# The split of the rows for hop 3, done by groups of five tiles inside the tail of the first feed-forward stage

## The chip, the core and the metric

The kernel runs on one core of a Trainium2 chip. The metric is the device time of one execution in microseconds (us). A core has TensorE (PE: products of 128x128 weights with a moving operand, into the banks of PSUM), VectorE (DVE), ScalarE (ACT), GpSimd (POOL) and SyncE (SP), which here issues nearly all transfers. Each engine works through its own instructions in the order in which they were written. What one engine needs of another it waits for on a counter, a semaphore.

## What is computed

Two layers of a network over a graph with 3125 nodes of 256 features and 53125 edges. Each layer adds to a stream x a hop over the graph and an attention, then a feed-forward part; the second layer's hop is a plain sum over neighbours. Cut to the place that matters, from the first layer's feed-forward to the second layer's first hop:

```python
x = x + L0_ffn(layernorm(x))          # two experts, GELU, then its own layernorm
xn = layernorm(x)
# second layer, on xn
agg = segment_sum(xn[src], dst)       # hop 3
h = (1 + eps1) * xn + agg
h = relu(relu(h @ W1a + b1a) @ W1b + b1b)
h = (1 + eps2) * h + segment_sum(h[src], dst)       # hop 4
gnn = relu(h @ W2a + b2a) @ W2b + b2b
mix = linear_attention(rmsnorm(xn) @ w_qkv)          # queries and keys pass a softmax
x = x + gnn + mix
x = x + L1_ffn(layernorm(x))          # six experts
```

## The kernel before

**Tiles.** The nodes are cut into T = 25 tiles of 128 rows, and these into five groups of GROUP = 5 tiles. X holds the stream, N the normalised rows (both tile by tile), NT the normalised rows transposed.

**The end of the feed-forward stage.** TensorE runs the second expert products group by group (line 972, 80 matrix instructions a group, 16 a tile), into two PSUM banks in turn (the object V over TV). VectorE empties a bank with an addition into N (`accumulate`, line 1699) and by that gives it back. VectorE's loop at line 1808 is the tail, with steps s = 0 to 6. In step s it normalises group s - 2 into N (`normalised`, counted by `xn_ready`), empties group s's banks, takes group s - 1 through a layer norm and into the stream (`into_stream`, four parts between the five emptyings) and makes group s's statistics. Each layer norm needs a root of ScalarE, which VectorE asks for at the end of a step.

**Transposes.** `normalised_transposed(2, g)` on TensorE turns the five tiles of group g through three PSUM banks (TA). ScalarE copies each into NT (line 1208, counted by `nt_ready`) and then rounds the group to bf16 into hi16 (`leading_part`, line 1269, counted by `hi_ready`). Groups 0 and 1 are turned between the expert products, groups 2 to 4 at line 980, all of them before hop 3.

**The split.** Hop 3 is a dense product with an adjacency matrix in bf16; to keep fp32's accuracy each row is the sum of three bf16 parts: hi16, and two parts in both16, which lies over N itself. For tile t VectorE subtracts hi16 from N into one of three buffers (`remainder`, line 1913, `rest_ready`), GpSimd casts that into both16 (line 774, `mid_ready`), and VectorE subtracts the cast and writes the last part (`low_part`, line 1905, `lo_ready`). Since both16 overwrites N, GpSimd first waits until N has gone to DRAM (`table_written[2]`, five stores of SyncE), until ScalarE has squared all rows for the attention's norms (`norm_asked`; line 1295, 25 squares, then a root at line 1299) and until all tiles are transposed. `split_rows` is one run over 25 tiles. Ahead of it VectorE scales NT into the sums' rows AT (line 1953) and adds N into X (line 1958).

**Hop 3.** `dense_products` runs 40 pieces: 8 slabs of target nodes by 5 groups of source tiles. A piece is two halves (c = 0, 1) of fifteen matrix instructions (line 1062), and needs the three parts of its group. Lists of steps, `beside_pieces`, are worked off between the halves: for tile t of the attention, queries, keys and values (line 990) beside piece t, and the turn of the normalised queries (line 997) beside piece t + 1. VectorE has a list of its own, by piece: the norms (`over_norm`, line 1825), the normalising of queries, and at each slab's end the addition of the two banks into AT (line 1933), on which TensorE's next slab waits. SyncE loads pieces into four buffers.

Two passages that set the order (SyncE's loads and stores, and GpSimd's waits):

```python
            for i in range(4):
                load_piece(i)
            for g in range(GROUPS):
                sp.wait_ge(xn_ready, 2 * T + (g + 1) * GROUP)
                load(sp, rows_of_table(2, g * GROUP, (g + 1) * GROUP), N[:, g * GROUP:(g + 1) * GROUP, :], table_written[2])
...
            pool.wait_ge(table_written[2], 16 * TABLE_DMAS[2])
            pool.wait_ge(norm_asked, 1)
            pool.wait_ge(nt_ready, 3 * T)
```

Of the kernel before, what the change touches and what calls it, by code (L numbers as in the profile page):

```python
# [29 lines left out]
ALU = mybir.AluOpType  # L30
# [25 lines left out]
GROUP = 5  # L56
# [55 lines left out]
def build(nc, a, out):  # L112
    with ExitStack() as ctx:
# [3 lines left out]
        def sem(name):  # L117
            return ctx.enter_context(nc.semaphore(name))
# [65 lines left out]
        table_sbuf = [sem(f"table_sbuf{h}") for h in range(4)]  # L184
        table_written = [sem(f"table_written{h}") for h in range(3)]
        row_stored = [sem(f"row_stored{i}") for i in range(4)]
        hidden_hi, hidden_rest, hidden_mid, hidden_lo = sem("hidden_hi"), sem("hidden_rest"), sem("hidden_mid"), sem("hidden_lo")
# [29 lines left out]
        def load(eng, dst, src, s):  # L217
            eng.dma_start(dst, src).then_inc(s, 16)
# [91 lines left out]
        V_B3 = V_GNN1 + T  # L310

        EARLY = 9
        A_W1B = A_MIX1 + 2 * T + 2 * SLICES * HC + EARLY
# [42 lines left out]
        def rows_of_table(i, first, last):  # L356
            return table[i][first * P:last * P, :].rearrange("(t p) d -> p t d", p=P)
# [13 lines left out]
        def _(sp):  # L371
# [38 lines left out]
            load(sp, beta_b, a["L0_ffn_beta"].partition_broadcast(P), b2_loaded)  # L410
            sp.wait_ge(pv_full, V_FFN0)
            load(sp, WA[:, 0:1024], a["w1a"], w1_loaded)
            sp.wait_ge(slab_stored, 16 * SLABS)
            def load_piece(i):
                load(sp, pieces[i % 4], adjacency[i // GROUPS][:, GROUP * (i % GROUPS):GROUP * (i % GROUPS + 1), :], piece_loaded[i % 4])

            for i in range(4):
                load_piece(i)
            for g in range(GROUPS):
                sp.wait_ge(xn_ready, 2 * T + (g + 1) * GROUP)  # L420
                load(sp, rows_of_table(2, g * GROUP, (g + 1) * GROUP), N[:, g * GROUP:(g + 1) * GROUP, :], table_written[2])
            for i in range(4, PIECES):
# [80 lines left out]
        def gather_general(pool, h):  # L503


            if h < 4:
                pool.wait_ge(table_written[h - 1], 16 * TABLE_DMAS[h - 1])
            else:
                for slot in range(4):
                    pool.wait_ge(row_stored[slot], 16 * len(range(slot, T, 4)))  # L510
# [217 lines left out]
        def _(pool):  # L728
# [39 lines left out]

            pool.wait_ge(table_written[2], 16 * TABLE_DMAS[2])
            pool.wait_ge(norm_asked, 1)  # L770
            pool.wait_ge(nt_ready, 3 * T)
            for t in range(T):
                pool.wait_ge(rest_ready, t + 1)
                nc.gpsimd.tensor_copy(both16[:, t, 0, :], remainder[:, t % 3, :]).then_inc(mid_ready, 1)
# [7 lines left out]
        def _(pe):  # L782
# [196 lines left out]

            for g in range(GROUPS - 3, GROUPS):  # L980
                normalised_transposed(2, g)
            pe.wait_ge(mix_sb, 7)
            pe.wait_ge(nt_ready, 3 * T)

            qkv_bank = [None]

            def queries_keys_values(t, c):
                if c == 0:
                    qkv_bank[0] = A.next()
                mm = nc.tensor.matmul(qkv_bank[0][:, 0:3 * HD1], NT[:, c, t * P:(t + 1) * P], wqkv[:, c, :],  # L990
                                      start=(c == 0), stop=(c == KC - 1))
                if c == KC - 1:
                    mm.then_inc(pa_full, 1)
# [37 lines left out]

            beside_pieces = {(i, c): [] for i in range(PIECES) for c in range(KC)}
            for t in range(T):
                for c in range(KC):
                    beside_pieces[t, c].append(lambda t=t, c=c: queries_keys_values(t, c))
            for t in range(T):
                beside_pieces[t + 1, 1].append(lambda t=t: turn_queries(t))
                beside_pieces[T + 10 + t // GROUP, int(t % GROUP > 1)].append(lambda t=t: attention_out(t))
# [58 lines left out]

            pe.wait_ge(at_ready, 1)
            dense_products()
# [89 lines left out]
        def _(act):  # L1189
# [75 lines left out]
            exp(sc[:, 0:8])  # L1265
            exp(sc[:, 40:41])
            def leading_part(g):
                act.wait_ge(xn_ready, 2 * T + (g + 1) * GROUP)
                nc.scalar.copy(hi16[:, g * GROUP:(g + 1) * GROUP, :], N[:, g * GROUP:(g + 1) * GROUP, :]).then_inc(hi_ready, 1)

            for g in range(GROUPS + 3):
# [17 lines left out]


            def squares(src, tiles, dump):

                for t in tiles:
                    st.settle()
                    st.add(nc.scalar.activation(dump, src[:, t, :], ACT.Square, accum_out=rn[:, t:t + 1]))

            def norms():
                st.settle()
                nc.scalar.activation(rn, rn, ACT.Sqrt).then_inc(norm_asked, 1)

            for g in range(GROUPS):
                squares(N, group(g), junk1)
            norms()
# [41 lines left out]

            act.wait_ge(table_written[2], 16 * TABLE_DMAS[2])
            act.wait_ge(at_ready, 2)
# [25 lines left out]
        def _(dve):  # L1373
# [415 lines left out]
            def into_stream(g):  # L1789
# [16 lines left out]
                yield  # L1806

            for s in range(GROUPS + 2):
                if s >= 2:
                    normalised(X, s - 2, xn_ready)  # L1810
                behind = into_stream(s - 1) if 1 <= s <= GROUPS else iter(())
                if s < GROUPS:
                    for t in group(s):
                        accumulate(N, [t])
                        next(behind, None)
                for _ in behind:
                    pass
                if s < GROUPS:
                    stats_of(N, s)


# [68 lines left out]

            beside_pieces = {t: lambda t=t: ([over_norm(1)] if t == 0 else []) + [normalise_queries(t)] for t in range(T)}
            beside_pieces[T] = key_maxima
# [5 lines left out]
            for g in range(GROUPS):  # L1898
                beside_pieces[T + 10 + g] = lambda g=g: [attention_in(t) for t in group(g)]

            def split_rows():

                def low_part(t):
                    dve.wait_ge(mid_ready, t + 1)
                    nc.vector.tensor_tensor(both16[:, t, 1, :], remainder[:, t % 3, :], both16[:, t, 0, :], ALU.subtract).then_inc(lo_ready, 1)

                for t in range(T):
                    if t % GROUP == 0:
                        dve.wait_ge(hi_ready, t // GROUP + 1)
                    if t >= 3:  # L1910
                        low_part(t - 3)
                        dve.wait_ge(lo_ready, t - 2)
                    nc.vector.tensor_tensor(remainder[:, t % 3, :], N[:, t, :], hi16[:, t, :], ALU.subtract).then_inc(rest_ready, 1)
                for t in range(T - 3, T):
                    low_part(t)

# [38 lines left out]
            dve.sem_inc(at_ready, 1)  # L1955
            for g in range(GROUPS):
                x, n = X[:, g * GROUP:(g + 1) * GROUP, :], N[:, g * GROUP:(g + 1) * GROUP, :]
                st.add(nc.vector.tensor_tensor(x, x, n, ALU.add))
            st.settle()
            split_rows()  # L1960
            dense_sums()
# [157 lines left out]
```

## Time and profile before

| | us |
|---|---|
| median of 3 runs | 3010.47 |
| lowest, highest | 3010.39, 3013.76 |
| the profiled execution, its time | 3010.55 |
| its span | 3008.8 |
| PE busy in the span | 2485.5 (83%) |
| DVE busy | 1299.6 (43%) |
| POOL busy | 867.6 (29%) |
| ACT busy | 454.3 (15%) |

The span is what the trace covers, from the first instruction to the last; the execution's time is a little longer. Times in the rows count from the span's start. The busy share of an engine is an average over stages with different limits; what holds up a stage is read from the waits in it. The granted clock (PEclk) is the share of TensorE's full 2.4 GHz that it was given in a stretch.

### The profile page before, as it was taken

How to read it: one execution, taken by the hardware profiler on the slowest of the kernel's cores; microseconds unless marked ns; L12 is line 12 of the kernel's file. 1: busy time of each engine (PE TensorE's matmuls, PEld its weight loads, DVE VectorE, ACT ScalarE, POOL GpSimd, SP SyncE). 2: the span in 40 equal slices, each digit the busy share in tenths (PEclk: the TensorE clock that was granted, in tenths of full speed). 3: DMA queues.
4: the chain of work that ended last, by engine and by line, in shares of the span. 5: the costliest groups of instructions: out<-in, count | busy, mean ns of one | idle time of the engine just before them, and what ended most of it. 6: DMA issues, size and time to landing. Idle time of an engine off the chain costs nothing.

```text
span 3008.8 us, 33687 instructions
## 1 busy us (share of the span) xinstructions
PE 2485.5 (83%) x12264; PEld 1717.6 (57%) x12264; DVE 1299.6 (43%) x3544; ACT 454.3 (15%) x963; POOL 867.6 (29%) x912
## 2 busy tenths in 40 slices
PE   4568777766666766689959998999999999999999
PEld 3456655654455555567735565565555557566665
DVE  8887867757665755532662224122000003131221
ACT  0211111101000000033231103330000010413222
POOL 0177777775777777220010000110000000000000
PEclk9988999987987888779979999999999999989999
DMA  3134344343434344110022221022111100000001
GB/s 104 58 100 136 103 138 139 105 136 113 137 107 138 105 138 139 37 36 1 32 76 69 70 70 43 32 76 79 49 55 51 36 1 0 22 11 11 11 11 43
DMA packets 77650, 211.87 MB, mean 70 GB/s; under 512 B 16445, under 2 KB 33845, under 8 KB 76073
## 3 DMA queue, kind: packets, MB, share of 16 engines
q0 software_dynamic: 40800, 111.47, 12.5%
q1 hardware_dynamic: 36681, 98.17, 9.9%
q8 instruction: 103, 1.69, 0.2%
q14 instruction: 66, 0.54, 0.1%
HBM read 169.10 MB, written 40.47 MB: 70 GB/s over the span
## 4 chain that ended last, share of the span: by engine, by line
PE 64%; DVE 15%; DMA 8%; issue 6%; POOL 3%; ACT 3%; DVEq 1%; SPq 0%; ACTq 0%; POOLq 0%
PE ps L1090 16%; PE ps L1127 13%; DMA rows<-table,src_i 8%; PE ps L1062 7%; PE ps L541 7%; PE ps L1185 4%; POOL rows L481 3%; PE ps L961 3%; PE ps L972 3%; DVE onehot L660 2%; DVE NN L1647 2%; DVE NN L1635 2%; PE ps L860 1%; DVE NN L1658 1%; PE ps L1147 1%
## 5 line engine op out<-in xcount | busy, mean ns | idle before, releaser
L481 POOL DMA_INDIRECT rows<-table,src_i x832 | 812.8, 977 | 388.6 <-issue 297.6
L541 PE MATMUL ps<-onehot,rows 128*128 128x128 f32 x3328 | 553.0, 308 | 222.9 <-DMA rows<-table,src_i 190.1
L541 PEld LDWEIGHTS ps<-onehot,rows 128*128 128x128 f32 x3328 | 519.2, 219 | 336.8 <-issue 236.2
L1090 PE MATMUL ps<-AS,WA 128*128 128x400 f32 (+1 forms) x768 | 259.8, 501 | 11.5 <-ACT NN L1329 5.0
L860 PE MATMUL ps<-NN 128*128 128x500 bf16 x416 | 168.0, 404 | 106.8 <-DVE NN L1636 94.3
L660 DVE TENSOR_SCALAR onehot<-iota_w,rel,wgt 128x128 f32<-128x128 f32 x848 | 230.9, 361 | 2.8 <-DVE iota_w L700 1.6
L1090 PEld LDWEIGHTS ps<-AS,WA 128*128 128x128 f32 x768 | 148.5, 194 | 121.5 <-issue 6.0
L1090 PE MATMUL ps<-NN,WA 128*128 128x400 f32 (+1 forms) x640 | 213.6, 495 | 1.0 <-ACT rows L1342 0.7
L2057 DVE SCALAR_TENSOR_TENSOR X<-ps,WA,X 128x256 f32<-128x256 f32 x150 | 72.5, 484 | 272.2 <-PE ps L1185 272.2
L1329 ACT ACTIVATE AS<-ps,small 128x400 f32<-128x400 f32 (+1 forms) x224 | 131.2, 586 | 334.8 <-PE ps L1090 334.8
L1090 PEld LDWEIGHTS ps<-NN,WA 128*128 128x128 f32 x640 | 122.0, 191 | 89.3 <-issue 1.6
L2001 DVE SCALAR_TENSOR_TENSOR AS<-ps,small,AS 128x408 f32 x32 | 20.3, 643 | 347.3 <-PE ps L1127 346.5
L678 DVE TENSOR_TENSOR AS<-AS,ps 128x256 f32 x104 | 43.8, 421 | 282.1 <-PE ps L541 282.1
L1647 DVE TENSOR_TENSOR NN<-NN,ps 128x500 f32 x208 | 140.1, 674 | 50.7 <-issue 22.5
L1635 DVE TENSOR_SCALAR NN<-WB,AS 128x500 bf16<-128x500 f16 x416 | 150.0, 360 | 0.3
L1127 PE MATMUL ps<-WA,NN 128*128 128x408 bf16 x768 | 137.1, 336 | 0.0
L1127 PE MATMUL ps<-onehot,NN 128*128 128x408 bf16 x768 | 136.1, 336 | 0.0
L1185 PE MATMUL ps<-WA,AS 128*128 128x256 f32 x600 | 135.7, 388 | 0.0
L1185 PEld LDWEIGHTS ps<-WA,AS 128*128 128x128 f32 x600 | 104.1, 191 | 31.6 <-issue 13.2
L860 PEld LDWEIGHTS ps<-NN 128*128 128x128 bf16 x416 | 43.7, 105 | 129.7 <-DVE NN L1647 87.1
L1636 DVE TENSOR_SCALAR NN<-WB,AS 128x128 bf16<-128x128 f16 x416 | 117.7, 283 | 0.0
L778 POOL CAST rows<-WA 128x512 bf16<-128x512 f32 x5 | 4.7, 932 | 384.7 <-DVE WA L1980 384.7
(353 smaller groups left out, 3077.2 us busy)
## 6 DMA issues: line engine op xcount, KB each, us to landing
adjacency<-NN SPq DMA_DIRECT2D x8, 2550.0 KB, 9.2
onehot<-adjacency SPq DMA_DIRECT2D x40, 510.0 KB, 3.5
WA<-adjacency SPq DMA_DIRECT2D x40, 510.0 KB, 3.5
rows<-table,src_i POOLq DMA_INDIRECT x832, 2.8
table<-NN SPq DMA_DIRECT2D x10, 640.0 KB, 3.3
table<-WA SPq DMA_DIRECT2D x25, 256.0 KB, 2.0
WA<-in_experts SPq DMA_DIRECT2D x6, 768.0 KB, 4.2
X<-in_x SPq DMA_DIRECT2D x1, 3072.0 KB
```

The source lines that it names most:

```text
L481: nc.gpsimd.indirect_dma_start(slot_of(h, j, k), None, table[h - 1][:, :], bass.IndirectOffsetOnAxis(index, 0)).then_inc(gathered[h - 1][( ...
L541: mm = nc.tensor.matmul(EDGE[j % 2][:, c * P:(c + 1) * P], row[:, c * P:(c + 1) * P], onehot[:, j % 2 * U + k, :], start=(k == 0 and c == ...
L660: nc.vector.tensor_scalar(onehot[:, buffer * U + k, :], iota_w[:, :], rel[:, bass.ds(c, 1)], wgt[:, bass.ds(c, 1)], ALU.is_equal, ALU.mult ...
L860: nc.tensor.matmul(build_bank(s)[:, 0:CELLS], sources_in[:, n % CELL_RING, :], cells[:, n % CELL_RING, :], start=(j == 0), stop=(j == 1)). ...
L1062: mm = nc.tensor.matmul(EDGE[c][:, 0:SLABW], rows16, pieces[i % 4][:, n, :], start=(t == 0 and part == 0), stop=(t == T - 1 and part == 2))
L1090: mm = nc.tensor.matmul(o[:, 0:n.stop - n.start], weights[:, k, c * P:(c + 1) * P], src[:, k, n], start=(k == 0), stop=(k == chunks - 1))
L1127: mm = nc.tensor.matmul(banks[c][:, 0:SLABW], hidden16(t)[:, part, f], pieces[i % 4][:, n, :], start=(t == 0 and part == 0), stop=(t == T ...
L1185: mm = nc.tensor.matmul(o[:, 0:D], h2[:, k, t * P:(t + 1) * P], w[:, 2, k, :], start=(k == 0), stop=(k == KC - 1))
L1329: nc.scalar.activation(dst[:, c, n], o[:, 0:n.stop - n.start], ACT.Relu, bias=bias[:, c:c + 1]).then_inc(pa_free, 1)
L1635: nc.vector.tensor_scalar(cells[:, n % CELL_RING, :], iota500, cell_of[:, n:n + 1], None, ALU.is_equal).then_inc(cells_ready, 1)
L1636: nc.vector.tensor_scalar(sources_in[:, n % CELL_RING, :], iota500[:, 0:P], source_in[:, n:n + 1], None, ALU.is_equal).then_inc(cells_read ...
L1647: nc.vector.tensor_tensor(part, part, build_bank(s)[:, 0:CELLS].rearrange("p (t n) -> p t n", n=SUBW), ALU.add).then_inc(slab_added, 1)
```

## The change

The 25 tiles are split in five groups, each as soon as its own five tiles are normalised, rounded, squared and stored. VectorE's `split_rows(g)` moves into the tail's steps 3 to 6 (group 4 behind them) and takes the addition of N into X with it. ScalarE squares a group's rows right behind its `leading_part`, and reports them with a new counter, `squared`. The five stores have a counter each, `group_stored`. GpSimd waits per group. SyncE stores groups 0 to 2 ahead of pieces 2 and 3 and loads w1a last. On TensorE the groups 3 and 4 are transposed behind pieces 0 and 2 of hop 3, and queries, keys and values of tiles 0 to 5 stand beside pieces 3 to 5, two tiles a piece (`piece_of`).

```diff
+        def piece_of(t):
+            return 3 + t // 2 if t < 6 else t
...
-            sp.wait_ge(pv_full, V_FFN0)
-            load(sp, WA[:, 0:1024], a["w1a"], w1_loaded)
...
-            for i in range(4):
-                load_piece(i)
-            for g in range(GROUPS):
+            def store_group(g):
                 sp.wait_ge(xn_ready, 2 * T + (g + 1) * GROUP)
-                load(sp, rows_of_table(2, g * GROUP, (g + 1) * GROUP), N[:, g * GROUP:(g + 1) * GROUP, :], table_written[2])
+                load(sp, rows_of_table(2, g * GROUP, (g + 1) * GROUP), N[:, g * GROUP:(g + 1) * GROUP, :], group_stored[g])
+
+            load_piece(0)
+            load_piece(1)
+            for g in range(3):
+                store_group(g)
+            sp.wait_ge(pv_full, V_FFN0)
+            load_piece(2)
+            load_piece(3)
+            for g in range(3, GROUPS):
+                store_group(g)
+            load(sp, WA[:, 0:1024], a["w1a"], w1_loaded)
...
-            pool.wait_ge(table_written[2], 16 * TABLE_DMAS[2])
-            pool.wait_ge(norm_asked, 1)
-            pool.wait_ge(nt_ready, 3 * T)
             for t in range(T):
+                if t % GROUP == 0:
+                    pool.wait_ge(group_stored[t // GROUP], 16)
+                    pool.wait_ge(squared, t // GROUP + 1)
+                    pool.wait_ge(nt_ready, 2 * T + t + GROUP)
...
-            for g in range(GROUPS - 3, GROUPS):
-                normalised_transposed(2, g)
-            pe.wait_ge(mix_sb, 7)
-            pe.wait_ge(nt_ready, 3 * T)
+            normalised_transposed(2, GROUPS - 3)
...
             beside_pieces = {(i, c): [] for i in range(PIECES) for c in range(KC)}
+            beside_pieces[0, 1].append(lambda: normalised_transposed(2, GROUPS - 2))
+            beside_pieces[2, 1].append(lambda: normalised_transposed(2, GROUPS - 1))
             for t in range(T):
                 for c in range(KC):
-                    beside_pieces[t, c].append(lambda t=t, c=c: queries_keys_values(t, c))
+                    beside_pieces[piece_of(t), c if t >= 6 else t % 2].append(lambda t=t, c=c: queries_keys_values(t, c))
+                if t >= 1:
+                    beside_pieces[piece_of(t), 1 if t >= 6 else t % 2].append(lambda t=t: turn_queries(t - 1))
+            beside_pieces[T, 1].append(lambda: turn_queries(T - 1))
...
             def leading_part(g):
                 act.wait_ge(xn_ready, 2 * T + (g + 1) * GROUP)
                 nc.scalar.copy(hi16[:, g * GROUP:(g + 1) * GROUP, :], N[:, g * GROUP:(g + 1) * GROUP, :]).then_inc(hi_ready, 1)
+                squares(N, group(g), junk1)
+                st.settle()
+                act.sem_inc(squared, 1)
...
+            def split_rows(g):
+                x, n = X[:, g * GROUP:(g + 1) * GROUP, :], N[:, g * GROUP:(g + 1) * GROUP, :]
+                dve.wait_ge(xn_ready, 2 * T + (g + 1) * GROUP)
+                st.do(nc.vector.tensor_tensor(x, x, n, ALU.add))
+                dve.wait_ge(hi_ready, g + 1)
+                for t in group(g):
+                    if t >= 3:
+                        if t - 3 >= g * GROUP:
+                            low_part(t - 3)
+                        dve.wait_ge(lo_ready, t - 2)
+                    nc.vector.tensor_tensor(remainder[:, t % 3, :], N[:, t, :], hi16[:, t, :], ALU.subtract).then_inc(rest_ready, 1)
+                for t in group(g)[-3:]:
+                    low_part(t)
...
                 if s < GROUPS:
                     stats_of(N, s)
+                if s >= 3:
+                    split_rows(s - 3)
+            split_rows(GROUPS - 1)
```

VectorE, between tail steps 3 and 4, before (NN is N, `ps` a PSUM bank, `small` the statistics):

```order
L1424 BN_AGGR small<-small 128x2 x5
L1426 TENSOR_SCALAR small<-small 128x5
L1416 RECIPROCAL small<-small 128x5
L1432 TENSOR_SCALAR NN<-X,small 128x256 x5
L1699 TENSOR_TENSOR NN<-NN,ps 128x256
L1416 RECIPROCAL small<-small 128x5
```

The same place with the change (line numbers are those of the changed kernel; WA holds the three remainders, `rows` is hi16):

```order
L1445 TENSOR_SCALAR small<-small 128x5
L1835 TENSOR_TENSOR X<-X,NN 128x1280
L1842 TENSOR_TENSOR WA<-NN,rows 128x256 x3
L1829 TENSOR_TENSOR NN<-WA,NN 128x256
L1842 TENSOR_TENSOR WA<-NN,rows 128x256
L1829 TENSOR_TENSOR NN<-WA,NN 128x256
L1842 TENSOR_TENSOR WA<-NN,rows 128x256
L1829 TENSOR_TENSOR NN<-WA,NN 128x256 x3
L1435 RECIPROCAL small<-small 128x5
L1451 TENSOR_SCALAR NN<-X,small 128x256 x5
L1718 TENSOR_TENSOR NN<-NN,ps 128x256
```

The addition into the stream and the ten subtractions of group 0 now stand between the statistics of group 3 and the first emptying of group 4's banks; the same for group 1 one step later, and so on.

TensorE, at the end of the feed-forward products (L972) and the start of hop 3 (L1062), before; L798 are the transposes:

```order
L961 MATMUL ps<-NN,WA 128x245 x2
L972 MATMUL ps<-WA,AS 128x256 x40
L798 MATMUL ps<-ident,NN 128x128 x10
L972 MATMUL ps<-WA,AS 128x256 x40
L798 MATMUL ps<-ident,NN 128x128 x40
L1062 MATMUL ps<-onehot,rows 128x408
```

With the change, the same rows:

```order
L976 MATMUL ps<-NN,WA 128x245 x2
L987 MATMUL ps<-WA,AS 128x256 x40
L813 MATMUL ps<-ident,NN 128x128 x10
L987 MATMUL ps<-WA,AS 128x256 x40
L813 MATMUL ps<-ident,NN 128x128 x20
L1081 MATMUL ps<-onehot,rows 128x408
```

And further down with the change, with the banks' numbers, from the end of piece 0 to the start of piece 1 (ps3 and ps4 collect hop 3's sums for c = 0 and 1, ps0 to ps2 take the transposes):

```order
L1081 MATMUL ps4<-onehot,rows 128x408
L1081 MATMUL ps4<-onehot,NN 128x408 x2
L813 MATMUL ps2<-ident,NN 128x128 x2
L813 MATMUL ps0<-ident,NN 128x128 x2
L813 MATMUL ps1<-ident,NN 128x128 x2
L813 MATMUL ps2<-ident,NN 128x128 x2
L813 MATMUL ps0<-ident,NN 128x128 x2
L1081 MATMUL ps3<-onehot,rows 128x408
```

Twenty of the forty transposes in front of hop 3 have moved into it: group 3's five tiles behind piece 0, and group 4's behind piece 2.

## Rows read from the trace of the kernel before

**Rows 1.** Waits of TensorE, 1490 to 1860 us: line, for whom, total, times, longest

```profile
PE ps L1062 <- DVE NN L1905: 20.4, 1, 20.4
PE ps L1062 <- DVE AS L1933: 17.2, 5, 3.5
```

**Rows 2.** Timeline of TensorE: start, length, instruction, count, idle time before and its releaser

```profile
1478.57 17.43 PE L972 MATMUL ps<-WA,AS 128*128 128x256 f32 x80
...
1510.93 2.60 PE L798 MATMUL ps<-ident,NN 128*128 128x128 f32 x10 [7.79 <-ACT NN L1208]
...
1556.20 0.48 PE L997 MATMUL ps<-ident,WA 128*128 128x128 f32 x1 [4.39 <-DVE WA L1840]
...
1582.45 0.50 PE L1062 MATMUL ps<-onehot,rows 128*128 128x408 bf16 x1 [3.39 <-DVE AS L1933]
...
1590.67 0.34 PE L1062 MATMUL ps<-WA,rows 128*128 128x408 bf16 x1
```

**Rows 3.** Timeline of ScalarE: casts of groups 0, 1 and 4, squares, root

```profile
1480.03 1.26 ACT L1269 CAST rows<-NN 128x1280 bf16<-128x1280 f32 x1
...
1498.68 1.26 ACT L1269 CAST rows<-NN 128x1280 bf16<-128x1280 f32 x1
...
1516.42 1.26 ACT L1269 CAST rows<-NN 128x1280 bf16<-128x1280 f32 x1
1517.59 0.41 ACT L1295 ACTIVATE AS<-NN 128x256 f32<-128x256 f32 x1
...
1531.09 0.23 ACT L1299 ACTIVATE small<-small 128x25 f32<-128x25 f32 x1
```

**Rows 4.** Timeline of VectorE: tail steps 3 to 5, sums' rows, split, norms

```profile
1479.81 0.17 DVE L1426 TENSOR_SCALAR small<-small 128x5 f32<-128x5 f32 x1
1481.43 0.19 DVE L1416 RECIPROCAL small<-small 128x5 f32<-128x5 f32 x1 [1.46 <-ACT small L1198]
...
1483.28 0.42 DVE L1699 TENSOR_TENSOR NN<-NN,ps 128x256 f32<-128x256 f32 x1
...
1500.08 0.19 DVE L1416 RECIPROCAL small<-small 128x5 f32<-128x5 f32 x1 [1.17 <-ACT small L1198]
...
1510.12 0.17 DVE L1426 TENSOR_SCALAR small<-small 128x5 f32<-128x5 f32 x1
...
1512.53 0.40 DVE L1945 MEMSET wgt<- 128x415 f32 x1
...
1517.85 7.10 DVE L1958 TENSOR_TENSOR X<-X,NN 128x1280 f32<-128x1280 f32 x5
...
1533.37 0.50 DVE L1913 TENSOR_TENSOR WA<-NN,rows 128x256 f32<-128x256 f32 x1
...
1534.66 0.41 DVE L1905 TENSOR_TENSOR NN<-WA,NN 128x256 bf16<-128x256 f32 x1
...
1552.39 0.17 DVE L1825 TENSOR_SCALAR small<-small 128x25 f32<-128x25 f32 x1
```

**Rows 5.** Timeline of GpSimd: the first casts of the split

```profile
1531.45 1.27 POOL L774 CAST NN<-WA 128x256 bf16<-128x256 f32 x3 [195.94 <-ACT small L1299]
1533.06 0.53 POOL L774 CAST NN<-WA 128x256 bf16<-128x256 f32 x1 [0.34 <-DVE WA L1913]
```

**Rows 6.** Chain of work that ended last, in order of time: start, length, what

```profile
1556.67 5.10 PE ps L1062 x15
...
1562.56 2.59 PE ps L1062 x15
1565.15 0.65 PE ps L990 x2
...
1582.45 4.40 PE ps L1062 x15
```

**Rows 7.** Busy time by stretch: length, five engines, granted clock, DMA share, GB/s

```profile
1536.09:1541.14 5.05, 5.05 (x15) 2.42 (x16) 4.88 (x12) 0.00 (x0) 3.02 (x7) 0.50 0.00 0
```

**Rows 8.** DMA issues, 1250 to 1520 us: transfer, queue, count, size, time to landing

```profile
table<-NN SPq DMA_DIRECT2D x5, 640.0 KB, 10.5
```

More of the change, by code:

```diff
@@ L185, in build @@
         table_written = [sem(f"table_written{h}") for h in range(3)]
+        group_stored = [sem(f"group_stored{g}") for g in range(GROUPS)]
+        squared = sem("squared")
         row_stored = [sem(f"row_stored{i}") for i in range(4)]
@@ L506, in gather_general @@
             if h < 4:
-                pool.wait_ge(table_written[h - 1], 16 * TABLE_DMAS[h - 1])
+                for g in range(GROUPS):
+                    pool.wait_ge(group_stored[g], 16)
             else:
@@ L977, in _ @@
             assert V.n == V_FFN0 and GROUPS > 4
-            for g in range(GROUPS - 3, GROUPS):
-                normalised_transposed(2, g)
-            pe.wait_ge(mix_sb, 7)
-            pe.wait_ge(nt_ready, 3 * T)
+            normalised_transposed(2, GROUPS - 3)
             qkv_bank = [None]
             def queries_keys_values(t, c):
+                if t == 0 and c == 0:
+                    pe.wait_ge(mix_sb, 7)
+                    pe.wait_ge(nt_ready, 3 * T)
                 if c == 0:
@@ L1032, in _ @@
             beside_pieces = {(i, c): [] for i in range(PIECES) for c in range(KC)}
+            beside_pieces[0, 1].append(lambda: normalised_transposed(2, GROUPS - 2))
+            beside_pieces[2, 1].append(lambda: normalised_transposed(2, GROUPS - 1))
             for t in range(T):
                 for c in range(KC):
-                    beside_pieces[t, c].append(lambda t=t, c=c: queries_keys_values(t, c))
+                    beside_pieces[piece_of(t), c if t >= 6 else t % 2].append(lambda t=t, c=c: queries_keys_values(t, c))
+                if t >= 1:
+                    beside_pieces[piece_of(t), 1 if t >= 6 else t % 2].append(lambda t=t: turn_queries(t - 1))
+            beside_pieces[T, 1].append(lambda: turn_queries(T - 1))
             for t in range(T):
-                beside_pieces[t + 1, 1].append(lambda t=t: turn_queries(t))
                 beside_pieces[T + 10 + t // GROUP, int(t % GROUP > 1)].append(lambda t=t: attention_out(t))
@@ L1096, in wide @@
                 return ends
-            pe.wait_ge(at_ready, 1)
             dense_products()
@@ L1266, in _, with squares @@
             exp(sc[:, 40:41])
+            def squares(src, tiles, dump):
+                for t in tiles:
+                    st.settle()
+                    st.add(nc.scalar.activation(dump, src[:, t, :], ACT.Square, accum_out=rn[:, t:t + 1]))
             def leading_part(g):
@@ L1269, in leading_part @@
                 nc.scalar.copy(hi16[:, g * GROUP:(g + 1) * GROUP, :], N[:, g * GROUP:(g + 1) * GROUP, :]).then_inc(hi_ready, 1)
+                squares(N, group(g), junk1)
+                st.settle()
+                act.sem_inc(squared, 1)
             for g in range(GROUPS + 3):
@@ L1288, in _ @@
             leading_part(GROUPS - 1)
[L1291 to L1295, printed above, removed]
             def norms():
@@ L1299, in norms @@
                 nc.scalar.activation(rn, rn, ACT.Sqrt).then_inc(norm_asked, 1)
-            for g in range(GROUPS):
-                squares(N, group(g), junk1)
             norms()
@@ L1344, in hidden_rows @@
                     act.sem_inc(hidden_hi, 1)
-            act.wait_ge(table_written[2], 16 * TABLE_DMAS[2])
+            for g in range(GROUPS):
+                act.wait_ge(group_stored[g], 16)
             act.wait_ge(at_ready, 2)
@@ L1806, in into_stream, with low_part @@
                 yield
+            def low_part(t):
+                dve.wait_ge(mid_ready, t + 1)
+                nc.vector.tensor_tensor(both16[:, t, 1, :], remainder[:, t % 3, :], both16[:, t, 0, :], ALU.subtract).then_inc(lo_ready, 1)
+            def split_rows(g):
[11 more added lines that the diff above has]
+                    low_part(t)
             for s in range(GROUPS + 2):
@@ L1889, in attention_in @@
                 nc.vector.tensor_tensor(Y[:, t, :], V.next()[:, 0:D], bout_b, ALU.add).then_inc(pv_free, 1)
-            beside_pieces = {t: lambda t=t: ([over_norm(1)] if t == 0 else []) + [normalise_queries(t)] for t in range(T)}
+            beside_pieces = {piece_of(t): lambda t=t: normalise_queries(t) for t in range(6, T)}
+            for i in range(3):
+                beside_pieces[3 + i] = lambda i=i: ([over_norm(1)] if i == 0 else []) + [normalise_queries(2 * i), normalise_queries(2 * i + 1)]
             beside_pieces[T] = key_maxima
@@ L1899, in _ @@
                 beside_pieces[T + 10 + g] = lambda g=g: [attention_in(t) for t in group(g)]
[L1901 to L1915, printed above, removed]
             def dense_sums():
@@ L1955, in _ @@
             dve.sem_inc(at_ready, 1)
[L1956 to L1960, printed above, removed]
             dense_sums()
```

## The prediction, made before the changed kernel ran

> **What bounds the kernel now.** I read three views: the waits of TensorE in the stretch where the first feed-forward stage ends and hop 3 runs, then the timelines of the five engines around that place, then the chain of work that ended last. TensorE does nothing for 20.4 us before hop 3's first product, waiting for VectorE's subtractions, the split [rows 1]. Its feed-forward products end at 1496.0 (1478.57 + 17.43) [rows 2]; hop 3 starts at 1536.09 [rows 7]. In between stand twenty transposes in a row, of which the last groups wait 7.79 us for ScalarE [rows 2]. One piece later TensorE waits another 4.39 us for the first normalised queries [rows 2], because the split runs to 1552.39, where VectorE turns to the norms [rows 4]. After hop 3 everything follows TensorE, so what this place gains reaches the end of the span, and nothing else of the change does.
>
> **The change part by part.** No arithmetic is added: 25 squares, 25 pairs of subtractions, 25 casts and five additions into the stream are done in five groups. What counts is a chain through four engines, so I carry the times of the trace along it.
>
> *The feed-forward tail pays first.* VectorE ends tail step 3 at 1479.98 and now does the split of group 0 there, ahead of step 4. The split waits for GpSimd's casts, and these wait for all five squares of the group. ScalarE starts the bf16 cast at 1480.03 and the first square 1.17 later (1516.42 to 1517.59); a square takes 0.54 (13.50 over 25), five 2.7 [rows 3]: done at 1483.9. GpSimd starts 0.15 after, and the fifth low part ends 3.62 after that (1531.45 [rows 5] to 1534.66 + 0.41 [rows 4]): 1487.7. Step 4 then begins at 1487.7, not at 1481.43 [rows 4], 6.2 late, and with it the first emptying of a bank of group 4, from 1483.70 (1483.28 + 0.42) to 1489.9. There are two such banks. TensorE's third tile of this group wants the first one back at 1478.57 + 2 x 3.49 = 1485.5 (17.43 over five tiles [rows 2]), so it stands still for 4.4 us inside a stage that never waited. The gap costs more than itself: after 4.39 us idle, fifteen products of hop 3 took 5.10 instead of 2.59, after 3.39 us 4.40 [rows 2, 6]; at hop 3's start, after the longest idle stretch, the granted clock is 0.50, the 1.2 GHz level [rows 7]. I take 2.5, the row with the nearer gap. The feed-forward stage ends at 1502.9, **6.9 us later**. Ends of this term: 0 if the bank comes back in time, and about 15 if all three tiles (10.5) run at the lower level.
>
> *From there to the end of the split.* Group 1's cast stood 2.68 after the products' end (1498.68) [rows 3]; now it starts at 1505.6, its squares end 1.17 + 2.7 later, 1509.5, and the split of group 1 ends 0.15 + 3.62 later, at 1513.2. VectorE's step 5 takes 10.2 (1500.08 to 1510.12 + 0.17) [rows 4]: 1523.4. TensorE starts piece 0 at about 1511, as soon as ScalarE has copied out enough of group 2, some 25 us earlier than before. Behind it, however, stand the transposes of group 3: three fill the banks and the fourth needs ScalarE, which first owes VectorE a root that step 5 asks for at its end. In the kernel before that same wait ended 0.64 after the step (1510.29 to 1510.93 [rows 2, 4]). So piece 0 gains nothing by itself: the two last transposed tiles end at 1523.4 + 0.64 + 1.04 (four of ten transposes in 2.60 [rows 2]), 1525.1. Piece 1 follows an idle stretch, hence 5.10 + 2.59, to 1532.8; piece 2 takes 2 x 2.59, to 1538.0 [rows 6]. The split of group 2 (under 6 us after 1523.4, its squares being long done) is not what piece 2 waits for. Then group 4 is transposed: cast 2.68 later, squares 3.9 more, at 1544.6, the split of group 4 ends at 1548.3. VectorE has split group 3 by then, about 1537, so piece 3 isn't held.
>
> *What still lies behind the split.* VectorE then clears and scales the sums' rows (1512.53 to 1517.85, 5.3 [rows 4]), and from its norms to the first turned queries 3.8 pass (1552.39 [rows 4] to 1556.20 [rows 2]): 1557.4. The change lets that turn stand at the end of piece 3, which is done at about 1548, so a wait of about 9 us takes the place of the 4.39. Piece 4 starts at 1557.7; in the kernel before piece 2 started at 1556.5. Two pieces are won, 2 x 6.5, but queries, keys and values of two tiles are still to do. Pieces 4 and 5 carry two tiles each; a half of one is 0.65 [rows 6]. Piece 4: 5.10 + 2.59 + 4 x 0.65 and two short turns, 10.5, to 1568.2. At the first slab's end the 3.4 us wait [rows 2] stays, with its latency 3.5, since the queries of piece 4's last tile are normalised ahead of the sums. Piece 5: 8.2 as before (1582.45 to 1590.67 [rows 2]) plus 1.4: it ends at 1581.3. Piece 6 then starts there instead of at 1590.67, **9.4 us earlier**, and from there both kernels do the same.
>
> *Edits at nothing.* The additions into the stream (7.10 together [rows 4]) now stand before the waits for the squares in groups 0, 1 and 4, and so are covered there; without that cover they cost 1.4 each. SyncE puts three of the five stores ahead of pieces 2 and 3 and of the wait for the feed-forward's end. A store landed 10.5 us after issue in the crowd of before [rows 8]; group 4's, asked at about 1531, would land by 1541.5, and GpSimd wants it at 1544.6. Piece 4's load is queued behind that store and w1a, and has some 25 us. Were a store late, its lateness would add in full to the chain.
>
> Sum: 3010.55 (the profiled execution, within 0.1 of the median 3010.47) - 9.4 = **3001.2 us**.
>
> **The rivals.**
> (A) *The tail covers its split.* If VectorE gets back to group 4's bank before TensorE wants it, the 6.9 isn't paid and the whole chain moves up: 16.3 us gained, 2994.3. For it: the stage before shows eighty products in a row without a wait [rows 2], so VectorE was ahead there. Against: the third tile's wait follows from two banks and 6.2 us of lateness.
> (B) *Given back inside the chain.* It has a dozen handoffs between engines; a few tenths more on each, or one or two further half pieces at the lower clock (2.5 each), leave 3 to 6 us of gain: about 3006, not to be told from no change. For it: hop 3 now begins in short bursts with waits between them. Against: every handoff above is read with its latency.
> (C) *Slower: the clock does not come back.* TensorE is interrupted in the feed-forward stage, before piece 1, and before pieces 4 and 5. If it stayed at 1.2 GHz from the gap on, the three tiles cost 8 more and the rest of pieces 1, 2, 4 and 5 some 19 more: 3010.55 - 9.4 + 27 = 3028. It ends above the time before from about four half pieces on. Against: the clock was at 0.50 for one half piece [rows 7], and a half piece after each later gap took 2.59 again [rows 6].
> (D) *The split is slower under two engines.* In the trace a cast of GpSimd, 0.53 from 1533.06, lies across a VectorE subtraction of 0.50 from 1533.37, and neither waits for the other's end [rows 4, 5]; the pace is one tile in 0.87. Had cast and subtractions to take turns, a tile would cost 0.53 + 0.50 + 0.41 = 1.44; over the 15 tiles of the three groups on the chain 8.6 us more: 3009.8. The Trainium skill, "SBUF — State Buffer", section "Who interferes with whom", says that a VectorE instruction with two SBUF inputs contends with a GpSimd instruction that reads SBUF, and its summary of rules that the later one blocks until the first is done. The overlap in these rows does not bear out full blocking, so D has a small chance.
>
> **How the numbers follow.** Forecast 0.60, A 0.10, B 0.21, C 0.07, D 0.02. A difference of 0.2%, 6 us, is about what a measurement can tell from no change. Faster takes the forecast and A, 0.70; same takes B and D, 0.23; slower takes C, 0.07. The range reaches down to A's time, 2994. Upwards it takes in piece 1 wholly at the lower clock (3003.7), that with another half piece and B's 3006, up to 3008; D and C are left out.
>
> **What would show it.** In the profile after: one wait of TensorE of about 4.4 us for VectorE inside the last group of the feed-forward products, which end near 1503; the first piece near 1511; a wait for ScalarE's copies after piece 0, ending near 1524; a wait of about 9 us at the first turned queries, ending near 1557; piece 6 near 1581.3; and from there on the same lengths. The prediction is wrong if no wait stands in the feed-forward stage (then A), if piece 2 waits for a split, or if pieces 4 to 6 run at half clock.

## The result, and the profile after

The changed kernel takes **2996.62 us** (median of 5, 2993.78 to 2999.50) against 3010.47 (5 runs, 3009.15 to 3014.27): a ratio of 0.9950, interval 0.9940 to 0.9961. It is 13.9 us faster; 9.3 were forecast. The profiled execution took 2993.78, its span is 2992.0.

Waits of TensorE in the same stretch as in [rows 1] (engine, line, releaser: us in total, times, longest). The 20.4 us for the split are gone; in their place stand one wait in the feed-forward products (line 987), two for ScalarE's copies (line 813) and one of 10.1 at the first turned queries (line 1012):

```profile
PE ps L1081 <- DVE AS L1960: 17.2, 5, 3.5
PE ps L1012 <- DVE WA L1881: 10.1, 1, 10.1
PE ps L813 <- ACT NN L1226: 9.3, 2, 5.0
...
PE ps L987 <- DVE NN L1718: 4.2, 1, 4.2
```

The timeline of TensorE there, which answers to [rows 2] (start, us, line, shape, count, idle time before and its releaser):

```profile
1478.80 7.07 PE L987 MATMUL ps<-WA,AS 128*128 128x256 f32 x32
1490.12 12.31 PE L987 MATMUL ps<-WA,AS 128*128 128x256 f32 x48 [4.25 <-DVE NN L1718]
1509.76 1.14 PE L813 MATMUL ps<-ident,NN 128*128 128x128 f32 x4 [4.22 <-ACT NN L1226]
1510.70 0.55 PE L1081 MATMUL ps<-onehot,rows 128*128 128x408 bf16 x1
1523.50 1.15 PE L813 MATMUL ps<-ident,NN 128*128 128x128 f32 x4 [5.04 <-ACT NN L1226]
1556.16 0.47 PE L1012 MATMUL ps<-ident,WA 128*128 128x128 f32 x1 [10.06 <-DVE WA L1881]
1570.75 0.33 PE L1081 MATMUL ps<-onehot,rows 128*128 128x408 bf16 x1 [3.40 <-DVE AS L1960]
1578.72 0.34 PE L1081 MATMUL ps<-WA,rows 128*128 128x408 bf16 x1
```

Piece 6 starts at 1578.72, where it started at 1590.67 before [rows 2]: **11.95 us** are won at this place. But the span is 16.8 shorter. The other 5 come from stretches that the change doesn't touch. In the chain of work that ended last, of the changed kernel, these are the first half pieces behind the hand-overs from slab to slab (fifteen products; a row with x30 takes in the half piece behind it), and further on fifty products of line 1034 with the thirty behind them:

```profile
1570.75 2.75 PE ps L1081 x15
...
1608.63 4.09 PE ps L1081 x15
...
1646.79 4.43 PE ps L1081 x15
...
1684.95 4.42 PE ps L1081 x15
...
1723.11 6.70 PE ps L1081 x30
...
1775.34 5.76 PE ps L1034 x50
1781.62 8.12 PE ps L1081 x30
```

and the same in the kernel before (the first hand-over is in [rows 6]: 4.40):

```profile
1620.57 4.11 PE ps L1062 x15
...
1658.41 5.26 PE ps L1062 x15
...
1697.80 4.43 PE ps L1062 x15
...
1735.96 7.02 PE ps L1062 x30
...
1788.52 8.50 PE ps L1019 x50
1797.53 6.94 PE ps L1062 x30
```

Code and waits are the same, the durations aren't: 2.75 to 5.26 for fifteen products that take 2.59 at full clock [rows 6]. The fifty products of line 1034 (1019 before) and the thirty behind them stand behind no such wait; together they took 13.88 and 15.44. Two later places differ likewise, the first products of hop 4 and the second wide layer's. In the timeline of TensorE, of the changed kernel:

```profile
2040.49 11.91 PE L1145 MATMUL ps<-onehot,rows 128*128 128x408 bf16 x60 [3.91 <-DVE AS L2023]
2406.74 84.24 PE L1109 MATMUL ps<-AS,WA 128*128 128x400 f32 x256 [2.44 <-DVEq L2030]
```

and of the kernel before, behind the same idle times:

```profile
2054.47 13.36 PE L1127 MATMUL ps<-onehot,rows 128*128 128x408 bf16 x60 [3.91 <-DVE AS L2001]
2422.17 85.88 PE L1090 MATMUL ps<-AS,WA 128*128 128x400 f32 x256 [2.45 <-DVEq L2008]
```

It is the granted clock. Windows of 4 us from these two places in each kernel (length in us, busy time of PE, PEld, DVE, ACT, POOL with counts, then the granted clock, DMA share, GB/s), the changed kernel first:

```profile
2040.49:2044.49 4.00, 4.00 (x16) 1.89 (x17) 1.50 (x3) 0.00 (x0) 0.00 (x0) 0.64 0.00 0
2406.74:2410.74 4.00, 4.00 (x12) 2.38 (x13) 0.00 (x0) 0.59 (x1) 0.00 (x0) 1.00 0.02 6
```

```profile
2054.47:2058.47 4.00, 4.00 (x12) 1.77 (x13) 1.50 (x3) 0.00 (x0) 0.00 (x0) 0.50 0.00 0
2422.17:2426.17 4.00, 4.00 (x7) 2.23 (x8) 0.00 (x0) 0.00 (x0) 0.00 (x0) 0.58 0.02 6
```

Counted from the start of the last feed-forward group's products (1478.57 before [rows 2], 1478.80 after; I call this start **the mark**), the sum is: 11.9 up to the second slab's first product (103.9 against 92.0), 0.1 lost over the next two slabs, 3.1 from the fourth slab to the first wide products, 0.75 lost there, 1.45 at hop 4, 1.64 at the second wide layer, 0.3 lost behind: 17.0. The mark itself came 0.2 later.

### The profile page after: what moved, and what is told of

It is laid out like the page before. It is cut to its first block, busy times and chain, and to the rows that moved or that the text cites. A ratio compares the mean times of both kernels' runs of the same rounds, so it can differ in the third digit from the quotient of the medians.

```text
span 2992.0 us, 33704 instructions
## 1 busy us (share of the span) xinstructions
PE 2478.4 (83%) x12264; PEld 1717.7 (57%) x12264; DVE 1299.7 (43%) x3544; ACT 454.3 (15%) x963; POOL 866.6 (29%) x912
## 4 chain that ended last, share of the span: by engine, by line
PE 63%; DVE 15%; DMA 8%; issue 6%; POOL 5%; ACT 2%; DVEq 1%; SPq 0%; ACTq 0%; POOLq 0%
PE ps L1109 16%; PE ps L1145 13%; DMA rows<-table,src_i 8%; PE ps L1081 7%; PE ps L555 6%; POOL rows L494 5%; PE ps L1203 5%; PE ps L976 3%; PE ps L987 3%; DVE onehot L674 2%; DVE NN L1666 2%; DVE NN L1654 1%; PE ps L875 1%; PE ps L1165 1%; PE ps L813 1%
```

## Experiments

**How they are read.** The mark moves by some microseconds from one execution to the next, 1477.9 to 1484.7 in the traces of the changed kernel and its variants. From the mark to the end of the span the same kernel repeats to 0.3 us, in the two pairs of traces that there are (after and a0, c23 twice). So each kernel has numbers that its median, with a scatter of 3 us, can't give: the time from the mark to the first turned queries, where the chain of the prediction ends, to the second slab's first product, and to the end.

| kernel | first turned queries after the mark | second slab after the mark | end after the mark | median, us | ratio |
|---|---|---|---|---|---|
| before | 77.6 | 103.9 | 1530.2 | 3010.5 to 3014.6 | 1 |
| after | 77.4 | 92.0 | 1513.2 | 2996.6 | 0.9950 |
| a0_change (the same) | 77.4 | 92.0 | 1513.3 | 2995.2 | 0.9936 |
| e1_split0_in_step4 | 77.0 | 90.1 | 1516.7 | 2997.1 | 0.9948 |
| e2_turn4_behind_piece1 | 72.7 | 86.2 | 1513.2 | 2995.2 | 0.9941 |
| e3_scale_behind_queries | 73.2 | 86.5 | 1513.4 | 2993.1 | 0.9939 |
| e4_squares_twice | 86.4 | 99.9 | 1526.7 | 3010.1 | 0.9986 |
| e5_turn_all_first | 77.6 | 89.2 | 1513.2 | 2997.9 | 0.9938 |
| c23_both | 68.5 | 80.2 | 1503.0 | 2984.7 | 0.9903 |
| c123_all | 67.8 | 79.6 | 1506.4 | 2991.0 | 0.9922 |
| f1_c123_delay3 | 67.9 | 79.7 | 1503.1 | 2984.8 | 0.9906 |
| f2_after_delay17 | 77.3 | 91.8 | 1519.8 | 3002.8 | 0.9967 |
| f3_e2_delay4 | 72.7 | 86.2 | 1509.7 | 2993.0 | 0.9933 |
| c23_again | 68.5 | 80.2 | 1502.7 | 2984.0 | 0.9901 |

At the first turned queries the kernel before has two pieces done, all the others four. The theory of the first eight runs is the prediction's chain through VectorE, ScalarE and GpSimd; the rivals are that hop 3's early start is itself the gain, or that the chain's steps don't matter.

**a0_change.** 

> The changed kernel as it is, as the reference point of the others on the same chip. Both theories: 2996.6 us, 13.9 us under the kernel before. In the profile: a gap of about 4.2 us in the last feed-forward group, a wait of about 10 us at the first turned queries, piece 4 about 96.5 us after the first product of that last group (1478.80 to about 1556.5 in the first profile).

2995.18 us, ratio 0.9936 (0.9923 to 0.9950). In another set of runs, the same lengths from the mark, to 0.1.

**The first split moved out of tail step 3.**

```diff
-                if s >= 3:
+                if s == 4:
+                    split_rows(0)
+                if s >= 4:
                     split_rows(s - 3)
```

> The split of group 0 stands at the end of tail step 4, right ahead of group 1's, not at the end of step 3. Chain theory: the gap in the feed-forward products goes, they end 6.1 us earlier, but the two splits now stand one behind the other (5.7 us each, squares done by then), so group 1's split ends only about 2 us earlier, and piece 4 and the time with it: 2994.6 us. Rival, the gap in the products costs what it measures (4.25 of standing still and 1.85 at the lower clock): 2990.5 us. Second rival, the gap costs nothing since TensorE waits later anyway: 2996.6 us.

The timeline of TensorE shows the wait in the feed-forward stage gone but for 0.89, and the time spent again one step later, at the copies that wait behind VectorE's step 5:

```profile
1490.43 10.63 PE L987 MATMUL ps<-WA,AS 128*128 128x256 f32 x48 [0.89 <-DVE NN L1718]
...
1526.47 1.14 PE L813 MATMUL ps<-ident,NN 128*128 128x128 f32 x4 [8.26 <-ACT NN L1226]
```

The products end 5.0 us earlier after the mark, but that wait for the copies ends only 0.7 earlier (44.0 against 44.7 after the mark), and the first turned queries come 0.3 earlier. So nearly all of the 4.25 us wait in the feed-forward stage costs nothing: TensorE has to wait for the end of VectorE's step 5 in either case. The chain was forecast to give 2 and gave 0.3. The second slab does start 1.8 earlier, but 1.5 of this is the clock in piece 4: behind waits of 10.06 us in both kernels its first fifteen products took 5.10 in the changed kernel and 3.82 here, by the chain of work that ended last, the changed kernel first:

```profile
1556.63 5.10 PE ps L1081 x15
```

```profile
1559.96 3.82 PE ps L1081 x15
```

The median, 2997.09, is not better than a0's; 2994.6 was forecast, a miss.

**Group 4's transposes behind piece 1 instead of piece 2.**

```diff
-            beside_pieces[2, 1].append(lambda: normalised_transposed(2, GROUPS - 1))
+            beside_pieces[1, 1].append(lambda: normalised_transposed(2, GROUPS - 1))
```

> The transposes of group 4 stand behind piece 1 and not behind piece 2. Chain theory: they can start at 1531.4 instead of 1536.5 (the rows are normalised at 1530.5), so the split of group 4 and the first turned queries come 5.2 us earlier, the wait there falls from 10 to about 5 us: 2991.4 us. Rival, TensorE's own work up to piece 4 is the bound and the wait for the queries is only where its slack shows: no change, 2996.6 us.

**VectorE's scaling of the sums' rows (5.3 us) behind the first queries.** The loop of line 1980 becomes a function that is called after `beside_pieces[3]`.

> VectorE scales the sums' rows behind the first two tiles' queries instead of ahead of them. Chain theory: 4.2 us leave the chain between the split of group 4 and the first turned queries, and fall into VectorE's idle 5.7 us before the next queries: the wait at the turn falls from 10 to about 6 us, 2992.4 us. Rival, TensorE's own work is the bound: 2996.6 us. Second rival, the scaling then stands in front of the next queries or of the first slab's sums and is given back: 2996.6 us, with the slab's wait longer than 3.4 us.

Both shorten the wait at the first turned queries, 5.43 and 5.84 us instead of 10.06. First the one with earlier transposes, then the one with later scaling:

```profile
1553.02 0.48 PE L1012 MATMUL ps<-ident,WA 128*128 128x128 f32 x1 [5.43 <-DVE WA L1881]
```

```profile
1551.07 0.48 PE L1012 MATMUL ps<-ident,WA 128*128 128x128 f32 x1 [5.84 <-DVE WA L1881]
```

The first turned queries come 4.7 and 4.2 us earlier after the mark, where the chain says 5.2 and 4.2. The second slab starts 5.8 and 5.5 earlier; the difference is the clock again, with 4.22 and 4.07 us for piece 4's first fifteen products instead of 5.10. The medians, 2995.24 and 2993.08, show 0 and 2 against a0's: the end after the mark is where it was.

**The squares doubled.** Each group's five squares on ScalarE are issued twice.

> ScalarE squares each group twice, 2.7 us more a group, the first result being overwritten by the same. Chain theory: the squares of groups 0, 1 and 4 stand on the chain, those of groups 2 and 3 beside VectorE's work: 8.1 us more, 3004.7 us; the gap in the feed-forward products grows from 4.2 to about 6.9 us. Rival, only the squares of the last group count, as the others are behind the feed-forward stage or behind pieces: 2.7 us more, 2999.3 us. Second rival, all hidden: 2996.6 us.

```profile
1498.68 12.77 PE L987 MATMUL ps<-WA,AS 128*128 128x256 f32 x48 [6.95 <-DVE NN L1719]
...
1571.06 0.48 PE L1012 MATMUL ps<-ident,WA 128*128 128x128 f32 x1 [12.77 <-DVE WA L1882]
```

The wait in the feed-forward stage grows from 4.25 to 6.95, by 2.7, exactly five squares (0.54 each [rows 3]), and so do the wait for ScalarE's copies ahead of piece 0, from 4.22 to 6.91, and the wait at the queries: one wait for each of the groups 0, 1 and 4. The first turned queries come 9.0 later (8.1 forecast; the rest is the clock, 12.77 instead of 12.31 for the three tiles and 12.50 instead of 12.04 for pieces 1 and 2), the second slab 7.9, the end 13.5: the squares are on the chain, but 5.6 us came on top behind it.

**All transposes before hop 3 again.** The two entries in `beside_pieces` are taken out, and groups 2 to 4 are turned in a row.

> All transposes stand ahead of hop 3, as in the kernel before; everything else is the change. Piece 0 then starts near 1533 instead of 1510.7. Chain theory: the early start of pieces 0 to 2 only fills a wait; without it the split of group 4 ends about 5 us earlier, TensorE does not wait at the first turned queries and keeps its clock, and piece 4 starts within 3 us of the changed kernel's: 2996 to 2999 us. Rival, the early start of hop 3 is what the change gains by: pieces 0 to 2 (18 us with the slow first half) come back onto the path, 3008 to 3011 us.

No piece runs before the split's last group is transposed: hop 3 starts 52.7 us after the mark, in the changed kernel 31.9. And yet the second slab starts 2.7 us earlier than in the changed kernel, and the end is the same to 0.1. The early start of hop 3 is not what gains. That the earlier end of the split is, e2 and e4 bear out: they moved it, and the first turned queries with it.

**Both edits, and all three.**

> Group 4 turned behind piece 1 and the scaling behind the first queries, together. Chain theory: 9.4 us leave the chain, the wait at the first turned queries falls to about 1 us, so TensorE keeps its clock in piece 4 (2.5 us more): 2984.7 us. Rival, with the wait gone TensorE's own work binds and only one of the two counts: 2991 us.

> The same with the split of group 0 in tail step 4 as well. Chain theory: another 2 us: 2982.7 us. Rival, the feed-forward gap pays in full: 2978.6 us. Second rival, no difference to the two together: 2984.7 us.

c23 has the second slab 11.7 us earlier and takes 2984.65 us, 0.9903 (0.9888 to 0.9918); TensorE arrives at the first turned queries almost together with them:

```profile
1546.73 0.33 PE L1012 MATMUL ps<-ident,WA 128*128 128x128 f32 x1 [1.19 <-DVE WA L1881]
```

With the first edit added, the second slab is another 0.7 earlier, and the end 3.4 us later after the mark (6 in the medians). Something behind hop 3's first slab answers to more than its start.

**What is open, and the second theory.** Up to here the chain was right in place, to a microsecond at the first turned queries, in e2, e3, e4 and c23, and 1.7 us too high in e1; at the end it was wrong in e1, e2, e3, e4 and c123. The ten traces so far fall into two patterns behind the fourth slab's first product: to the first wide products 188.4 us in after, a0, e5 and c23, and 191.1 to 191.5 in before, e1, e2, e3, e4 and c123; at hop 4's first sixty products 11.9 or 13.4; at the second wide layer 84.2 or 85.9. From the fourth slab's first product to the end the first take 1345.1 to 1345.3 us, the others 1350.4 to 1351.0. Two theories: *timing*, that the moment at which the later waits begin decides where the clock falls; or *order*, that something in these edits costs time later. They part if nothing but a delay is added. Products that are issued once more, with the first one's operands, before the second half of the second slab's first piece are such a delay (3, 17 and 4 of them, 0.172 us each):

```diff
+                        for _ in range(3 if i == GROUPS and c == 1 else 0):
+                            nc.tensor.matmul(EDGE[c][:, 0:SLABW], hi16[:, 0, f], pieces[i % 4][:, 0, :], start=True, stop=True)
                         for n in range(GROUP):
```

> The kernel of c123_all with three products of the second slab's first piece, second half, issued once more (3 x 0.17 us, 0.5 us in all, on TensorE's chain, behind the wait for the first slab's sums). What is compared is the stretch from the start of the last feed-forward group to the end of the span: 1513.2 us in the changed kernel, 1503.0 in c23_both, 1506.4 in c123_all. Timing theory (where the granted clock falls depends on when each later wait begins, so a local gain is partly taken back or doubled afterwards): the wait for the second slab's sums then ends 119.6 us after that start, where c23_both had it, and everything behind runs as in c23_both: 1503.0, that is 3.4 us SHORTER with more work. Rival (the early split itself costs something later): 0.5 us longer, 1506.9. By medians: about 2987.5 against 2991.5.

> The changed kernel with seventeen products of the second slab's first piece issued once more (17 x 0.172, 2.9 us). Timing theory: the waits behind the next slabs come 2.9 us later and fall into the pattern that six of the ten profiled kernels show (the kernel before among them), which costs 3 us behind the fourth slab's wait and 1.5 and 1.7 us behind two later ones, less 2 between: the stretch from the last feed-forward group to the end grows from 1513.2 to 1520. Rival (a delay is a delay): 1516.1. By medians: 2995.4 plus 6.8 or plus 2.9.

> The kernel of e2_turn4_behind_piece1 with four products of the second slab's first piece issued once more (0.7 us). Timing theory: the wait for the second slab's sums ends 126.4 us after the start of the last feed-forward group instead of 125.7, the wait for the third's at 164.6 instead of 162.2, and the clock then stays up behind the later waits as in the changed kernel: the stretch to the end is 1509.8 us instead of 1513.2, 3.4 SHORTER with more work, and the 5.8 us that the earlier transposes gain in place would for once reach the end in good part. Rival: 0.7 longer, 1513.9. By medians: about 2992 against 2996.

> The kernel of c23_both once more beside these, on one chip: the stretch from the last feed-forward group to the end is again 1503.0 us by the timing theory, whatever the time at which that group starts; about 2985 in the median, ratio to the kernel before 0.990 to 0.991. f1_c123_delay3 should come out level with it by the timing theory, 3.9 us slower by its rival.

All four lengths came out as the timing theory has them: 1503.1, 1519.8, 1509.7 and 1502.7 for 1503.0, 1520, 1509.8 and 1503.0. f1 does 0.5 us more work than c123 and is 3.3 us shorter from the mark (2984.8 and 2991.0 in the medians, of different sets of runs); f3 does 0.7 more than e2 and is 3.5 shorter. A delay of 2.9 us in the changed kernel costs 6.6. f1 and c123 differ by the three products alone; windows from the first product of their third and of their fifth slab, c123 first:

```profile
1600.85:1604.85 4.00, 4.00 (x22) 2.29 (x23) 0.40 (x1) 0.00 (x0) 0.00 (x0) 1.00 0.00 0
1675.10:1680.10 5.00, 5.00 (x15) 2.30 (x16) 0.40 (x1) 0.00 (x0) 0.00 (x0) 0.50 0.00 0
```

```profile
1601.77:1605.77 4.00, 4.00 (x16) 2.12 (x17) 0.41 (x1) 0.00 (x0) 0.00 (x0) 0.65 0.00 0
1678.09:1683.09 5.00, 5.00 (x18) 2.40 (x19) 0.41 (x1) 0.00 (x0) 0.00 (x0) 0.66 0.00 0
```

The waits before all four are 3.45 us; what differs is the moment, 0.65 us after the mark at the third slab. There f1 is the slower (4.12 us for the first fifteen products, against 2.75), at the fifth slab the faster (4.40 against 5.26). Against the changed kernel f2 has 5.26 instead of 4.42 at the fifth slab, and 13.43 instead of 11.91 for hop 4's first sixty products. From the fourth slab's first product to the end f1, f3 and c23_again take 1345.1 to 1345.2 us, f2 1350.8: the two values again. The delay was made of products; one in which TensorE stands idle was not tried. c23 again, at 2983.98 us (0.9901, 0.9885 to 0.9918), and f1 beside it, at 2984.8, are the fastest versions found, some 10 us below the changed kernel from the mark.

## Why the prediction was right, and where it was off

**The chain held.** Forecast and measured: the casts of group 0, which stand behind the fifth square, at 1484.05 and 1484.27; the wait in the feed-forward stage 4.4 and 4.25; its end 1502.9 and 1502.43; group 3's last transposes done at 1525.1 and 1524.65; the wait at the first turned queries about 9 and 10.06, ending at 1557.4 and 1556.16. GpSimd and VectorE, in the timelines of their engines, at the first of these:

```profile
1484.27 1.27 POOL L789 CAST NN<-WA 128x256 bf16<-128x256 f32 x3 [148.52 <-ACTq L1296]
1485.88 0.53 POOL L789 CAST NN<-WA 128x256 bf16<-128x256 f32 x1 [0.34 <-DVE WA L1842]
```

```profile
1486.19 0.50 DVE L1842 TENSOR_TENSOR WA<-NN,rows 128x256 f32<-128x256 f32 x1
```

And the place where ScalarE's root holds the transposes, in the chain of work that ended last: VectorE's step 5 ends, the root, a copy, four transposes, then sixty products, pieces 1 and 2:

```profile
1522.68 0.18 DVE small L1445
1522.89 0.21 ACT small L1216
1523.10 0.27 ACT NN L1226
1523.50 1.15 PE ps L813 x4
1524.64 12.04 PE ps L1081 x60
```

**Three terms were too dear.** Each is a price of the clock. For the three tiles behind the 4.25 us wait I took 2.5; they took 12.31 instead of 10.46 (three times 3.49), 1.85. The end of the products came 0.47 earlier for it. For pieces 1 and 2 I took 12.87 (5.10 + 3 x 2.59); they took 12.04 in the chain above, since the lower clock did not last through the first half piece. The two bring the turned queries 1.24 earlier. For piece 5's first half 4.40, the row of the same hand-over before; it took 2.75, the clock not having fallen. 1.24 and 1.65, less some 0.3 in pieces 4 and 5, are the 2.55 by which the 9.4 in place became 11.95.

**The step that failed** is the last sentence of the sum, that from piece 6 on both kernels do the same, and with it the premise that what this place gains reaches the end of the span as it is. They issue the same, but the kernel before was in the dearer of the two patterns and the changed one in the cheaper, which is 5.1 of the 17.0 us after the mark. I had read the prices of the hand-overs from one trace as constants of those places. f2 shows what that was worth: moved by 2.9 us, the changed kernel gains 10.4 after the mark instead of 17.0, 2.9 of the loss being the delay and 3.7 the clock. Which pattern the changed kernel would fall into was not forecast; that it was the cheaper was luck.

**The rivals.** (A) did not occur: the wait stands in the feed-forward stage. But its price was wrong too. e1 removes 3.4 of the wait and brings 0.3 at the first turned queries and 1.8 at the second slab, not the 6.9 that I had put on it, since VectorE's split of group 0 only changes its place and step 5 ends 0.7 earlier. (B) is half true as a mechanism: e2 and e3 show gains of 5.8 and 5.5 us taken back in full, not in the chain of handoffs but by the clock behind later waits. (C) did not occur: behind each wait the half pieces came back to 2.59. (D) did not occur: the cast from 1485.88 to 1486.41 lies across the subtraction from 1486.19, as before. The edits put at nothing held: no group's first cast in the changed kernel waited for a store.

**The medians.** 13.9 (after) and 16.7 (a0, against 3011.9) both fit 17.0 within the scatter of the mark.

## What to carry to other kernels

Follow a change through its chain of handoffs and compare the two traces from a common mark just ahead of it: here that gave a step's effect to 0.3 us from one profile, where medians scatter by 3. Read the effect at the wait that the step moves; a half piece later the clock is in it (e1: 0.3 us there, 1.8 at the second slab). Expect the end to move by that effect plus or minus what the clock gives or takes behind the later waits; an edit that saves 5 us in place may show nothing, and is not to be thrown away for that, since c23 joins two such edits and keeps 10. Where TensorE waits at fixed places, try a small delay as well: half a microsecond of added products made one kernel 3.3 us shorter from the mark.

## What the runs showed of the hardware

The price of a wait of TensorE in granted clock isn't a property of its length. Behind the hand-overs, all of 3.39 to 3.46 us, the first half piece took between 2.75 and 5.26 us, and 2.59 is the time at the 2.4 GHz level; behind 10.06 us it took 5.10 or 3.82. The Trainium skill, "TensorE: Matmul & The Clock Gate", Part 1, has a hardware monitor set the clock by how busy TensorE has been. The rows agree in the main, as the lower level mostly stands behind idle time. In two places it doesn't: at the end of fifty products of line 1034 with one moving column each, and of fifty of line 1180 with six each, the clock fell while TensorE was busy throughout. Windows of the changed kernel around the first of them:

```profile
1778.00:1780.50 2.50, 2.50 (x24) 2.50 (x23) 0.00 (x0) 0.00 (x0) 0.00 (x0) 1.00 0.00 0
1780.50:1784.00 3.50, 3.50 (x13) 2.13 (x14) 1.07 (x6) 0.00 (x0) 0.00 (x0) 0.50 0.00 0
```

At the second the granted clock is 1.00 from 2567.2 to 2572.4 and 0.50 from 2572.4 to 2575.8, with TensorE busy in full. That equal waits behind equal work end in either level, by the moment at which they begin, the runs f1 to f3 show and no row of one trace could. What that moment is measured against was not tried and stays open. It is hardly the start of the span: c23 and c23_again repeat to 0.3 us from the mark, though the mark lies at 1478.25 in one and at 1479.46 in the other, while 0.65 us after the mark parted f1 from c123. Nor was it tried why the mark moves by up to 7 us between executions; the gathers of hops 1 and 2 lie ahead of it.
